# An attention and mixture-of-experts layer: transposed maxima and expert weights in another order on SyncE's DMA queue

## The reference

```python
def attention(q, k, v):                       # k = v = context
    Q, K, V = heads(rope(q) @ Wq.T + bq), heads(rope(k) @ Wk.T + bk), heads(v @ Wv.T + bv)
    p = softmax(einsum('bhqd,bhkd->bhqk', Q, K) / sqrt(8))     # 16 heads of 8
    return merge(einsum('bhqk,bhkd->bhqd', p, V)) @ Wo.T + bo
def experts(x):                               # 8 experts, 352 hidden, top 2
    xn = rms_norm(x, scale)
    scores = xn @ w_router.T
    ids, c = top2(scores), softmax(scores)[ids]
    return x + sum(c[e] * ((val_e(xn) * silu(gate_e(xn))) @ down_e) for e in ids)
x = x + tanh(g_xattn) * attention(layernorm(x), ctx, ctx)
x = x + tanh(g_ffn) * experts(layernorm(x))
```

## Time and profile before

| | us |
|---|---|
| median of 3 runs | 461.07 |
| the runs | 461.07, 465.58, 459.24 |
| the profiled execution | 464.52 |
| its span, from first to last instruction | 462.4 |

### The profile page before, as it was taken

One profiled execution on the slowest core, in us unless ns is written; L12 is line 12 of the kernel. 1 busy time (PEld: TensorE's weight loads), 2 busy tenths in 40 slices (PEclk: granted clock), 3 DMA queues, 4 the chain that ended last, 5 costly groups with the idle time before them and its releaser, 6 DMA issues. The chain is left out here.

```text
span 462.4 us, 13236 instructions
## 1 busy us (share of the span) xinstructions
PE 395.3 (85%) x3794; PEld 266.0 (58%) x3795; DVE 300.3 (65%) x1131; ACT 261.0 (56%) x582; POOL 251.5 (54%) x205
## 2 busy tenths in 40 slices
PE   7576998897989899898987799998598999999980
PEld 3233545564555556556555487775376767776860
DVE  5467588887699888978887555564254455545540
ACT  3231758785687778767767666643244445444530
POOL 3555124226266665565434476577665665666684
PEclk9856999998999999999889899999999999999996
DMA  6350513228269540604211423555343443334330
GB/s 189 81 123 14 135 48 105 82 68 224 78 160 273 139 129 26 180 28 132 74 36 42 110 72 50 80 72 102 48 53 49 59 56 50 43 53 51 32 33 0
DMA packets 57421, 39.06 MB, mean 84 GB/s; under 512 B 8819, under 2 KB 55158, under 8 KB 57366
## 3 DMA queue, kind: packets, MB, share of 16 engines
q1 hardware_dynamic: 43190, 28.47, 23.6%
q0 software_dynamic: 12736, 8.64, 13.6%
q10 hardware_dynamic: 1440, 1.25, 1.1%
HBM read 14.26 MB, written 11.75 MB: 56 GB/s over the span
## 5 line engine op out<-in xcount | busy, mean ns | idle before, releaser
L499 POOL DMA_INDIRECT out<-ys,yi x72 | 112.6, 1564 | 57.4 <-issue 34.0
L415 POOL DMA_INDIRECT slots_dram<-xr,slu x64 | 66.9, 1045 | 60.8 <-ACT pt L563 45.1
L808 DVE TENSOR_REDUCE nmx<-bank 128x4 f32<-128x512 f32 x128 | 81.8, 680 | 8.3 <-PE bank L1277 8.1
L563 ACT ACTIVATE pt<-bank 128x512 f32<-128x512 f32 x128 | 72.5, 594 | 15.5 <-PE bank L1290 14.5
L1532 PEld LDWEIGHTS bank<-wf_sb,hT 128*128 128x128 f32 (+1 forms) x432 | 55.9, 190 | 36.0 <-issue 32.6
L1532 PE MATMUL bank<-wf_sb,hT 128*128 (+1 forms) x432 | 62.3, 280 | 14.6 <-DVE hT L1145 14.1
L707 ACT ACTIVATE ys<-bank,yc 128x128 f32<-128x128 f32 x72 | 26.4, 367 | 76.2 <-PE bank L1532 74.6
L1135 DVE TENSOR_TENSOR hh<-sg,bank 128x352 f32<-128x352 f32 x72 | 37.3, 519 | 42.1 <-ACT sg L699 22.1
L1510 PE MATMUL bank<-wf_sb,xT 128*128 x144 | 55.9, 470 | 0.1
L1512 PE MATMUL bank<-wf_sb,xT 128*128 x144 | 55.0, 464 | 0.0
L1303 PE MATMUL bank<-pt,v 128*9 128x128 f32 x1024 | 49.9, 276 | 4.1 <-ACT pt L563 2.7
(11 more groups left out here) (170 smaller groups left out, 701.2 us busy)
## 6 DMA issues: line engine op xcount, KB each, us to landing
qs<-parts SPq DMA_DIRECT2D x48, 128.0 KB
ks<-parts SPq DMA_DIRECT2D x42, 128.0 KB
xs<-slots_dram SPq DMA_DIRECT2D x72, 66.0 KB, 1.9
wf_sb<-in_wup SPq DMA_DIRECT2D x8, 352.0 KB
x_sb<-in_x SPq DMA_DIRECT2D x8, 256.0 KB, 3.9
ctx_sb<-in_ctx_in SPq DMA_DIRECT2D x8, 256.0 KB, 4.4
out<-x_sb SPq DMA_DIRECT2D x8, 256.0 KB, 2.7
out<-ys,yi POOLq DMA_INDIRECT x72, 3.3
```

Of the source, the lines that this page charges most:

```text
L415: nc.gpsimd.indirect_dma_start(out=slots_dram, out_offset=bass.IndirectOffsetOnAxis(ap=slu[:, c % 2, k, kk:kk + 1], axis=0), in_=xr[:, c % ...
L499: nc.gpsimd.indirect_dma_start(out=out.rearrange("b s d -> (b s) d"), out_offset=bass.IndirectOffsetOnAxis(ap=yi[:, r:r + 1], axis=0), in_ ...
L563: nc.scalar.activation(pt[:, 4 * g:4 * g + 4, :], STB[g % 2][:, :].rearrange("p (h s) -> p h s", h=4), ACT.Exp, scale=SCORE_SCALE).then_in ...
L808: nc.vector.tensor_reduce(nmx[:, b % 2, at:at + 4], SB[g % 2][:, :].rearrange("p (h s) -> p h s", h=4), AX.X, ALU.max, negate=True).then_i ...
```

## The change

Three things move in the SyncE loop. At u = 0 the maxima of batch b+2 stand before the last three key copies of the stack, at u = 1 and 2 before the store and the loads. The weights leave the blocks with u = 0: they are issued behind the maxima in blocks 9, 10, 11, 13, 14, 15, 17 and 18, and are the last thing of their block. The other engines' programs are the same.

```diff
                 if u == 0 and there(c + 1):
                     stack_free(c + 1)
                     stack_q_high(c + 1)
+                    stack_q_low(c + 1)
+                    stack_k_high(c + 1)
+                if real(b + 2):
+                    maxima(b + 2)
+                if u == 0 and there(c + 1):
+                    stack_k_low(c + 1)
                 if u == 1 and there(c - 2):
                     store(c - 2)
                 if u == 2 and there(c + 4):
                     load_x(c + 4)
                     load_ctx(c + 4)
-                if u == 0 and there(c + 1):
-                    stack_q_low(c + 1)
-                    stack_k_high(c + 1)
-                    stack_k_low(c + 1)
-                if 8 <= b < 8 + E:
-                    ffn_weights(b - 8)
-                if real(b + 2):
-                    maxima(b + 2)
+                if u and 8 <= b and 3 * (c - 2) + u <= E:
+                    ffn_weights(3 * (c - 2) + u - 1)
```

## The result

| | before | changed |
|---|---|---|
| median of 20 runs, us | 461.11 | 465.28 |
| lowest and highest, us | 458.04, 465.58 | 460.92, 473.73 |
| ratio, with its 95% interval | | 1.0075 (1.0047 to 1.0103) |
| the profiled execution, us | 464.52 | 462.16 |
| its span, us | 462.4 | 460.1 |

The changed kernel is slower by 0.75%, some 3.5 us: within the 2% that was called no change, but on the other side of zero than forecast (459.2), and above the range (455.5 to 463.2).

What follows compares the result with a forecast made beforehand. The prediction took PE in the attention stage, waiting on SyncE's queue, as the bound. Terms -3.5 (block 10), +0.4 (block 6) and +1.2 (block 18) gave -1.9 us from the median 461.07: 459.2, range 455.5 to 463.2.

Steps and rivals of the forecast that it cites:

- The sum: Whole kernel: -3.5 at block 10, +0.4 at block 6, +1.2 at block 18, 0 elsewhere, together -1.9 us.
- the base: Starting point: median of 461.07 us, with block 10's loss of 3.87 us read from one profiled execution.
- What bounds the kernel: Attention stage: PE, busy 180.6 of 204.5 us; its waits for SyncE's DMAs are paid in time, 4.0 us for maxima.
- Block 10: Blocks 9 and 10: earlier maxima recover 3.87 us less 0.3, a gain of 3.5, or 2.4 if the clock falls.
- The exchange of stalls: Block 6: last three key copies end their issues 1.14 us later, so PE waits at L1277 instead of L1290.
- The landing of 1.8 us: Stacks: the last three key copies are usable 1.8 us after their issues end, from 1.14 plus one copy's 0.64.
- Block 6: Start of block 6: the wait for keys replaces the wait for maxima and costs 0.4 us more.
- the slower rival: Stack of block 16 comes late behind 864 KB of weights: place costs 4.4 us, total 462.4; chance 0.15.
- Block 18: Block 18: stack of block 16 goes out later behind block 15's weights; costs 1.2 us, at most 1.6.
- the first rival: Same as the slower rival: 1.7 us backlog from weights isn't regained, clock falls near block 18; chance 0.15.
- the cover of 0.35: Stack issued in block 0: last key copies usable at 57.8, needed at 58.15, so no cost was taken.
- The stack of block 20: Block 20's stack: said to lie between block 24, covered by 0.5 us, and block 0, by 0.35; taken at 0.

Runs made afterwards that it cites:

- a0: The changed kernel itself, run again on another chip beside the kernel before: ratio 1.0071 to before, median 483.1 us (before 482.0).
- a1: Kernel before with only the maxima of blocks with u = 0 moved ahead of the last three key copies: ratio 1.0040 to before, median 482.8 us.
- b1: The dose: changed kernel with two more 4 KB maxima copies ahead of the last three key copies of every stack: ratio 1.0256 to before, median 493.0 us.
- b3: Changed kernel with the weights in blocks 9, 10, 13, 14, 17, 18, 21 and 22, none right ahead of a stack: ratio 1.0034 to before.
- c1: Changed kernel, but ScalarE instead of SyncE issues the maxima of blocks with u = 0: ratio 1.0001 to before, median 483.2 us.
- s0: Kernel before cut behind the 32 blocks, without its second stage: median 273.9 us.
- s2: Kernel before, cut behind the 32 blocks, with only the u = 0 maxima moved ahead of the last three key copies: median 276.0 us.
- s8: Changed kernel cut behind the 32 blocks, on a second chip: median 277.4 us, against 274.3 for the cut kernel before there.
- d1: Kernel before with only the weights moved, to blocks 9, 10, 13, 14, 17, 18, 21 and 22: ratio 1.0012 to before, median 475.6 us.
- s3: Kernel before, cut behind the 32 blocks, with only the weights moved as in the change: median 273.6 us.
- s6: Kernel before, cut behind the 32 blocks, with only the weights moved, to blocks 9, 10, 13, 14, 17, 18, 21 and 22: median 274.5 us.
- s1: Changed kernel cut behind the 32 blocks, on the first chip of the cut runs: median 275.9 us, against 273.9 for the cut kernel before.
- a3: Kernel before with store, loads and the weights of blocks with u > 0 behind the maxima, u = 0 blocks unchanged: ratio 0.9959 to before.
- s7: Kernel before cut behind the 32 blocks, on the second chip of the cut runs: median 274.3 us.

## Why the prediction was wrong

**The step that failed: the price of the new pauses.** The sum had 0.4 for block 6 and 1.2 for block 18, both as waiting alone. In the profiles these two places cost 5.5 us. Up to the start of L1277 they cost 2.3 (1.0 and 1.3), not 1.6; behind it 3.2 (1.6 and 1.7), with the clock at half level, and that part stood in the sum at nothing. The second step is the base: the gain of 3.5 at block 10 was true of the one profile it was read from, and other executions of that order had less to gain.

**What bounds the kernel: right.** PE in the first stage, through SyncE's queue.

**Block 10: right for this profile.** The gain was forecast as 3.5 with the pair at 13.8 and a pause of 0.7 for the keys; it measured 3.6, 13.71 and 0.59, with full clock.

**The exchange of stalls: right in kind.** "The low keys now end their issues 1.14 later" and "a new stall takes the old one's place" is what the rows show at blocks 6, 10 and 18. The landing of 1.8 us measured 1.87 at block 6, 1.9 at block 10 and 2.5 at block 18, behind the weights.

**Block 6: mis-sized.** Forecast 0.4, measured 2.5. The pause itself is larger by a slow issue in the q copies (six took 4.82, not 4.32). But more is the clock: I priced a fall only for the pause of 2.79 in block 10 and for the slower rival, and none for the pauses that my own sum made, 84.4 - 83.26 = 1.1 at block 6 and 170.85 - 168.74 = 2.1 at block 18. The falls at 84.20 and 169.50 stand within 1 us of the ends of pauses of 1.59 and 1.77. The prediction's rows had pauses of 0.5 to 0.7 with the clock up and one of 2.8 with it down, and nothing between: the sum used the range between as if it were safe. Nor is a fall certain. Of 13 pauses of 1.1 us and more for these DMAs (in before, changed, a0, a1, b1, b3, c1, s0, s2 and s8) eight had the half level right behind them and five had not, c1's 1.90 among them. So what a pause costs in the median lies between its price with the fall and without. With the maxima ahead the pair of blocks 5 and 6 took 15.75, 14.33, 15.64, 13.79, 15.68 and 13.60 (changed, a0, a1, b3, s2, s8), with the maxima last 13.23, 13.43, 15.43, 13.21 and 13.56 (before, d1, s0, s3, s6): 1.0 more on the mean, over several chips, where the one profile has 2.5. The Trainium skill, "TensorE: Matmul & The Clock Gate", section "What's actually happening", says that the slow stretches of one kernel vary from run to run; the executions of the changed kernel in a0 and in the profile, on two chips, agree with it.

**Block 18: mis-sized.** Forecast 1.2, at most 1.6; measured 3.0. The pause itself, 1.77, was no longer than the 2.1 of the sum; what the sum lacked is again the clock. Where it stayed up, in a0, the pair took 14.72, which is 1.2 over the 13.48 of before. The backlog of the weights was taken as regained over twelve copies, and it isn't always: with weights ahead the keys were usable 2.0 us (a0), 2.5 (changed), 4.2 (s8), 4.7 (c1) and 5.2 (s3) after their last issue. That was the first rival's mechanism, given 0.15, and its sign, a clock fall near block 18, came; but it had 4.4 for the place and 462.4 for the time, and was too low as well. The Trainium skill, "DMA: Bandwidth & Descriptors", section "Queues, rings and completion order", has a semaphore's increment land only after the earlier writes of its engine. The windows of c1 agree in that the keys came late, but they show that the engines were also still moving data, so the rows don't part a late semaphore from late data.

**Block 2: the cover of 0.35 failed.** The low keys took 3.02 us to issue instead of 1.92, and the pause was 0.74; the pair of blocks 1 and 2 took 13.10 (51.20 to 64.30) where before it was 12.71. A slow issue stood there in the profiles of b1, s1 and s8 as well; in s2 the issues were quick and the pause was 0.75 all the same. A cover of a few tenths, made of the shortest issue times, is none.

**The base.** The sum was taken off one execution's waits. Part of the 3.87 us at block 10 isn't there in the usual execution: where the profiled before had a pause of 2.79, the order of before around that block had 1.67 (a3), 1.75 (s0) and 0.42 (s7) on other chips. What is missing there was a gain that the median of before already had: the pair of blocks 9 and 10 took 17.34 us in the profile, and 14.69 and 13.48 in s0 and s7, where the changed kernel's took 13.7 to 14.2. How much of the 3.87 that is on the first chip, the runs don't say.

The forecast sum of -1.9 compares with +2.5 of the first stage in the profile: -3.6 at block 10, +2.5 at block 6, +3.0 at block 18, +0.4 at block 2, and +0.2 of all the rest, in which the other clock falls of both sides are. The stack of block 20, taken at 0 without a row, cost nothing there, but a0 paused 1.03 us for it at block 22. What isn't settled: how the 3.5 us of the medians divide between keys, weights and clock, since the parts alone have intervals as wide as the effect; whether all of it arises in the first stage; and why the second stage of the two profiles differs by 3.9 us.

## What to carry to other kernels

When something moves ahead in a queue, whatever it passes is late by its issue time, and if both are needed by neighbouring instructions of one engine the stall changes its name and stays: here 4.0 us of waits for the maxima became 4.7 for the keys. Price each pause that your own sum leaves, with the clock down and with it up, and treat a cover shorter than one slow issue as none. A profile is one execution: where runs scatter by more than the effect, read both kernels by stage, and double the suspected cost, since the 8.9 us of the dose stood clear where the parts of the 3.5 did not.

## What the runs showed that was not expected

A stack of twelve 128 KB copies behind 864 KB of weights was usable anywhere from 2.0 to 5.2 us after its last issue, one without weights ahead 1.9 us after it. The issue of one such copy took 0.6 us, but six of the 90 stack copies in the profile of before took 1.1 to 2.2, and at block 0 a slow one was among the same three copies in one profile of the changed order after another, with s2 as the exception. Chips differed by more than any version here: the kernel before had medians of 461, 482, 482, 478, 481 and 477 us on six occasions. And two executions with the same pause of 1.6 us of PE went on at full and at half clock, while other stretches of half clock, like those at 222 and 239 us of before, stood behind no wait for a DMA.
